# A four-layer decoder on one core: first-pass score tiles stand behind each half of a pair's scores

## What is computed

```python
# layer 0: 32 values a head, layer 1: 64 (four key heads), layer 3: 16
scores = jnp.einsum('bhid,bhjd->bhij', q, k) / sqrt(d)     # layer 0 adds a term for position
att = jnp.where(causal_mask, scores, -inf)
att = jax.nn.softmax(att, axis=-1)
y = jnp.einsum('bhij,bhjd->bhid', att, v)
```

## Time and profile before

| | us |
|---|---|
| three timed runs, median | 3255.83 |
| lowest and highest of them | 3252.84, 3267.48 |
| profiled execution, span (no other time is given for it) | 3262.6 |
| layer 0 attention, stretch 140 to 508 | 368: PE busy 314.55, DVE 239.07 |
| layer 1 attention, stretch 1140 to 1660 | 520: PE busy 415.08, ACT 321.41, POOL 327.25, DVE 276.62 |
| layer 3 attention, stretch 2555 to 2868 | 313: PE busy 266.24, DVE 224.46 |

### The profile page before, as it was taken

One profiled execution on the slowest core, in us unless ns is written; L12 is line 12 of the kernel. 1 busy time (PEld: TensorE's weight loads), 2 busy tenths in 40 slices (PEclk: granted clock), 3 DMA queues, 4 the chain that ended last, 5 costly groups with the idle time before them and its releaser, 6 DMA issues. The chain is left out here.

```text
span 3262.6 us, 45065 instructions
## 1 busy us (share of the span) xinstructions
PE 2508.7 (77%) x15890; PEld 1399.0 (43%) x15890; DVE 1855.3 (57%) x5014; ACT 1480.5 (45%) x2984; POOL 996.1 (31%) x822
## 2 busy tenths in 40 slices
PE   6788885785667577888874669897776788859977
PEld 2323324564443233333352255564443333346666
DVE  6576655565645455555553558335432577656678
ACT  5334451453432156666641514224412355537876
POOL 1145561146347566666612300001101111101200
PEclk9889998897878789999986869997687799978989
DMA  3311101610444411111002210001000322114023
GB/s 112 94 43 42 42 2 36 229 54 19 125 154 101 108 47 46 35 41 46 17 15 67 34 39 1 10 4 30 14 1 33 74 28 28 16 48 123 1 78 104
DMA packets 186942, 174.52 MB, mean 53 GB/s; under 512 B 52777, under 2 KB 160042, under 8 KB 186462
## 3 DMA queue, kind: packets, MB, share of 16 engines
q1 hardware_dynamic: 172030, 153.84, 16.8%
q0 software_dynamic: 9408, 12.56, 2.5%
q10 hardware_dynamic: 5280, 5.24, 0.5%
HBM read 117.62 MB, written 57.40 MB: 54 GB/s over the span
## 5 line engine op out<-in xcount | busy, mean ns | idle before, releaser
L946 POOL TENSOR_TENSOR l1a_p_lo<-res,l1a_p_hi 128x1024 f16<-128x1024 f32 x192 | 311.9, 1643 | 177.2 <-ACT res L1187 177.2
L1196 ACT ACTIVATE l0a_probs<-ps 128x1024 f32<-128x1024 f32 (+1 forms) x192 | 145.5, 810 | 176.2 <-PE ps L1050 103.7
L1196 ACT ACTIVATE l3a_probs<-ps 128x1024 f32<-128x1024 f32 (+1 forms) x192 | 146.9, 809 | 143.3 <-PE ps L1050 116.2
L1186 ACT ACTIVATE l1a_p_hi<-ps 128x1024 f16<-128x1024 f32 x192 | 157.8, 822 | 110.9 <-PE ps L1050 82.8
L1047 PE MATMUL ps<-l1a_qs,l1a_ks 128*128 128x512 f16 (+3 forms) x768 | 167.7, 333 | 31.6 <-ACT res L1187 31.6
L1016 PE MATMUL ps<-l1a_ks,l1a_qs 128*128 128x512 f16 (+3 forms) x384 | 122.2, 347 | 78.7 <-DVE l1a_nmax L1221 33.0
L1218 DVE CUSTOM_DVE_ANT_0 l1a_masked<-ps,l1a_wide_mask 128x128 bf16<-128x128 f32 (+3 forms) x256 | 118.0, 490 | 103.1 <-PE ps L1016 100.9
L971 POOL TENSOR_TENSOR l0a_both<-l0a_probs 128x768 f32<-128x768 f32 (+2 forms) x96 | 154.7, 1633 | 46.3 <-PE ps L1088 46.0
L1187 ACT ACTIVATE res<-ps 128x1024 f32<-128x1024 f32 x192 | 158.1, 823 | 0.0
L1050 PE MATMUL ps<-mask_t,ident_b 128*128 128x128 bf16 x768 | 157.5, 225 | 0.0
L1218 DVE CUSTOM_DVE_ANT_0 l0a_masked<-ps,l0a_wide_mask 128x128 bf16<-128x128 f32 (+3 forms) x256 | 116.5, 489 | 68.0 <-PE ps L1016 67.3
(11 more groups left out here) (749 smaller groups left out, 6453.7 us busy)
## 6 DMA issues: line engine op xcount, KB each, us to landing
f_wf<-in_L_ffn_w_dram SPq DMA_DIRECT2D x16, 1024.0 KB
f_slots<-x0a_zeros SPq DMA_DIRECT2D x32, 256.0 KB, 3.4
f_xe<-f_slots SPq DMA_DIRECT2D x32, 256.0 KB, 3.0
f_ys<-f_y SPq DMA_DIRECT2D x32, 256.0 KB
l1a_qs<-l_q_h SPq DMA_DIRECT2D x64, 128.0 KB
d_wall<-in_L_ffn_W_dram SPq DMA_DIRECT2D x3, 2112.0 KB
l0a_qs<-l_q_h SPq DMA_DIRECT2D x32, 128.0 KB
l0a_ks<-l_k_h SPq DMA_DIRECT2D x16, 256.0 KB
```

Of the source, the lines that this page charges most:

```text
L946: pool.tensor_tensor(ph_lo[:, n % SLOTS, :, 0:w], probs[:, n % FULL, :, 0:w], ph_hi[:, n % SLOTS, :, 0:w], ALU.subtract).then_inc(s_["low_ ...
L1186: act.activation(ph_hi[:, n % SLOTS, :, 0:w], SB[n % 2][:, :, 0:w], ACT.Exp)
L1196: act.activation(probs[0:KR, n % SLOTS, 2 * pr:2 * pr + 2, 0:w], SB[x % 2][:, :, 0:w], ACT.Exp).then_inc(s_["exps"], 1)
```

## The change

A unit now has a place behind each half of each pair of scores (2 x `PR` places), one behind the values unless `split` is set (layer 1), and one behind the sums only where sums come, that is in layer 0 on even units. `scores` gets the items that go between its two halves. In the last unit, which has no scores ahead, the places of both halves are worked off in turn. Nothing is added to or taken from any engine's instructions.

```diff
-    def lay(self, PR, C, ones):
+    def lay(self, PR, C, split, paired):
...
-                parts += [(n, k, 2 * C * w1) for k in range(PR)] + [(n, PR, 4 * w)] + ([(n, PR + 1, 4 * w)] if ones else [])
+                parts += [(n, k, max(C * w1, 1)) for k in range(2 * PR)]
+                if not split:
+                    parts.append((n, 2 * PR, 4 * w))
+                if paired and n % 2 == 0:
+                    parts.append((n, 2 * PR + 1, 4 * w))
...
+    paired = not own_sums and G == 4
+    items, before, beside, rest = plan.lay(PR, C, split, paired)
...
-                def scores(n, pr):
+                def scores(n, pr, between):
...
+                        for a in between if half == 0 else ():
+                            item(a)
...
                     for pr in range(PR):
                         if n + 1 < U:
-                            scores(n + 1, pr)
-                        for a in beside[n][pr]:
+                            scores(n + 1, pr, beside[n][2 * pr])
+                        for a in beside[n][2 * pr + 1] if n + 1 < U else beside[n][2 * pr] + beside[n][2 * pr + 1]:
                             item(a)
...
-                    for a in beside[n][PR]:
+                    for a in beside[n][2 * PR]:
                         item(a)
...
-                    for a in beside[n][PR + 1]:
+                    for a in beside[n][2 * PR + 1]:
                         item(a)
```

More of the change, by code:

```diff
@@ L808, in packed_attention @@
     n_ld = len(stack.q_parts) * GB + len(stack.k_parts) + (GB + 1 if q_pos is not None else 0)
-    items, before, beside, rest = plan.lay(PR, C, not own_sums)
+    paired = not own_sums and G == 4
+    items, before, beside, rest = plan.lay(PR, C, split, paired)
     turned_at = {s: a + 1 for a, (what, s, i) in enumerate(items) if what == "turn"}
@@ L819, in packed_attention @@
     invert_after = [[s for s in range(S) if s + INV < S and plan.first_unit[s + INV + 1] - 1 == n] for n in range(U)]
-    paired = not own_sums and G == 4
     in_reduce = plan.key_rows == P
@@ L1118, in _ @@
                 for pr in range(PR):
-                    scores(0, pr)
+                    scores(0, pr, ())
                 for n in range(U):
```

2 lines of the change are left out of this document (1 added, 1 removed).

## The result

The changed kernel is slower by about 1%: four executions with a median of 3286.99 us (3278.39 to 3302.34) against 3254.34 for the kernel before. The ratio is 1.0095, with a 95% interval of 1.0072 to 1.0118, so +23 to +38 us. The forecast was 3254, with a range up to 3268. The profiled execution is the shortest of the four (3278.39, span 3276.6), and that of the kernel before (span 3262.6) is some 10 us longer than its median, so the traces show less than the medians' 33 us: some 20 us in the four attentions, 14 in the span.

The account below looks back on a forecast made before the run. PE was taken as the fullest engine in the three causal attentions, its waits set by DVE and, in layer 1, also ACT. Layer 0 -7, layer 1 +7, layer 3 -2 made -2 us: 3255.8 to 3254, range 3240 to 3268.

Parts of the forecast that it names:

- the cover in layer 1's first part: Layer 1, odd turn to third tile: PE's path grows 1.2 us, costing nothing while SP's loads run; 1.1 us cover left.
- Rival (2): Layer 1, slower: the covered 2.0 us come through; 2 us a period more than counted gives 3284; chance 0.06.
- bound of 3.0 a period: Layer 1's upper bound if nothing covers: 0.5 + 1.2 + 0.8 + 0.5 = 3.0 us a period, +45 us.
- Second part of layer 1, +0.5: Layer 1, third tile to next odd turn: 0.46 + 0.3 - 0.6 + 0.5 - 0.2 = +0.5 us a period.
- The clock: Layer 1: four of 16 long waits drop the clock, 1.6 us each; half comes back, -3 us.
- Rival (3): Layer 1, slower: the split long wait drops the clock in each period, 11 more drops, 3275; chance 0.06.
- Layer 0, -7: Layer 0: -1.0 us a period over seven periods with tiles to place, -7 us.
- 0.27 + 0.83: Layer 0, gains a period: odd turn 0.27 us earlier, and 0.83 us saved by splitting five tiles behind the short step's values.
- Term (c): Layer 0: four tiles around sums instead of three, and long-step tiles meeting DVE mid-pair; +0.1 us, between 0 and +0.8.
- rival (4): Whole kernel: waits only change place and name because DVE's order and pace stay; 3256 +- 2; shares the forecast's chance 0.70.
- Layer 3, -2: Layer 3: odd turn 0.2 us and even turn 0.13 us earlier, 7 x 0.33 = -2 us, between -6 and +2.
- The tiling mode: Layer 1: a change from values to sums costs 0.1 us; as the only effect, -6 there and 3241 in all.

Follow-up runs that it names:

- run 5: The changed kernel with DVE's inverse ahead of the odd turn's split in layer 1, instead of behind it; 3273.55 us, ratio 1.0049.
- Runs 10: The kernel before, with layer 1's column transfer issued ahead of the last of the nine loads; 3254.40 us, ratio 1.0001.
- 11: The kernel before, with layer 1's column transfer issued ahead of the last three of the nine loads; 3232.16 us, ratio 0.9917.
- run 16: New places in layers 0 and 3, old ones in layer 1, loads behind the even step in all three, not the cross attention; 3213.37 us, ratio 0.9871.
- run 13: The kernel before, with new places only in the short steps of layers 0 and 3; 3254.23 us, ratio 0.9999.
- runs 14: New places in layers 0 and 3, old ones in layer 1, late loads in all three and the cross attention; 3237.54 us, ratio 0.9937.
- run 15: The kernel before with late loads alone, in layers 0, 1, 3 and the cross attention; 3239.71 us, ratio 0.9946.
- run 7: The kernel before, with layer 1's places all behind whole pairs, none behind halves, values or sums; 3305.63 us, ratio 1.0152.
- run 1: New places in layer 1 alone, layers 0 and 3 as in the kernel before; 3281.92 us, ratio 1.0073.
- run 2: New places in layers 0 and 3 alone, layer 1 as in the kernel before; 3250.68 us, ratio 0.9984.

## Why the prediction was wrong, point by point

**The step that failed is the cover in layer 1's first part.** The forecast had PE's path to the third tile grow by 1.2 us and let it cost nothing, because "that tile is released at 14.71 by SP's chain, which starts at the odd turn and is not touched". The path grew by 0.96 in run 5, where the stall is out (the tile at 15.14 us, less its wait of 1.80, against 14.71 less 2.33). But the tile is not released by SP's chain. The columns had landed by then (12.48 us behind the turn in the period shown), and the row that I quoted for them, already says that something else was late: 0.93 us for a sum of 128x8, which takes 0.15 behind the odd turn. It ends with POOL's subtraction, and that follows the exponentials, and they follow the scores ahead of the even turn, which TensorE's order delays. The cover moved along with what it was to cover. Runs 10 and 11 show it in the kernel before. In the changed kernel the rows show the same: the sum ends 0.02 us behind the subtraction in all 13 periods with loads, here in the period of the result (POOL ends at 1400.23, the sum at 1400.26):

```profile
1399.57 0.69 DVE L1249 TENSOR_TENSOR l1a_y_col<-l1a_y_col 128x8 f32<-128x8 f32 x1 [2.33 <-DMA l1a_y_col<-res]
```
```profile
1398.11 2.12 POOL L951 TENSOR_TENSOR l1a_p_lo<-res,l1a_p_hi 128x1024 f16<-128x1024 f32 x1 [2.47 <-ACT res L1194]
```

The table shows the consequence: the second piece of the period is the same to 0.03 us with and without the change. In the forecast's own cut, the first part was to stay at 14.71 us; it measured 15.87, and 15.14 without the stall.

**What the forecast did not have at all is the stall of 0.73 us** behind the odd turn. Its cause was in the sum: the odd turn 0.5 us later, which came out as 0.49. I counted it as half a microsecond on PE and did not ask which other engine's work starts by the clock of the scores and not of the turn. DVE's order was unchanged and so was POOL's, but their order against each other was not.

**The size.** 1.65 us a period by 15 periods are 24.8 us, which is what the profiled layer 1 lost (505.4 to 530.2). The forecast had +7. Rival (2) named the place and the price (2 us a period more than counted, 3284); it got a chance of 0.06 for want of a reason why the cover should fail. That the forecast's own terms with nothing covered, 0.5 + 1.2, come near 1.65 is luck: 0.73 of the loss is the stall, which is in neither. Its bound of 3.0 a period adds the turn's 0.8 to the 1.2, which by its own waits already holds it.

**Second part of layer 1, +0.5.** Cut at the third tile it measured 16.61 against 16.12, which is +0.49. So the sum of that part came out as forecast. But it is only the tile moving: from the even turn on, nothing was lost.

**The clock.** Half of four drops was to come back. Between the odd turns at 1222.67 and 1595.94 before, and 1220.82 and 1615.04 after, lie 12 periods; less 12 times the undisturbed period, drops cost 3.3 us before and 4.4 after. In this stretch there were eight instead of three, each cheaper (in the whole of layer 1's periods nine instead of four). Rival (3) thus had the right sign and a small part of the size, 1.1 us of its 18. Its price was also too high: the four drops of the kernel before made their periods 0.9 to 1.6 us longer, and the forecast read the dearest one.

**Layer 0, -7.** The short step did get shorter, 12.3 instead of 13.4 us, by as much as the 0.27 + 0.83 that I counted, though 0.43 of it is only moved, as follows. The long step got longer, from 27.6 to 28.2 to 29.2 us. Over six periods, odd turns from 225.11 to 471.29 before and from 229.01 to 475.22 after, the time is 246.18 and 246.21: nothing. Term (c), "+0.1, between 0 and +0.8", was the one mis-sized. Three things were not in it. The even turn now stands ahead of the last unit's values (0.43 us by their row), so a part of the gain only changed sides. DVE's waits do not go away when a bunch is taken apart: in the long step from 282.13 to 311.31 seven tiles wait for DVE. And SP's loads stand ahead of the columns in layer 0 as well, so the columns keep their distance from the odd turn: their transfer is issued 8.85 us behind it before (274.93) and 8.79 us now (278.60). With the shorter step the even turn comes before they land, and DVE, which had found them there, stands still for them (the changed kernel, and run 16, where the loads are late):

```profile
284.43 0.25 DVE L1252 RECIPROCAL l0a_r_col<-l0a_y_col 128x16 f32<-128x16 f32 x1 [1.39 <-DMA l0a_y_col<-l0a_sums]
```
```profile
282.93 0.23 DVE L1256 RECIPROCAL l0a_r_col<-l0a_y_col 128x16 f32<-128x16 f32 x1
```

PE's first wait of that long step hangs on it:

```profile
285.76 0.39 PE L1021 MATMUL ps<-l0a_ks,l0a_qs 102*128 102x512 f16 x1 [0.59 <-DVE l0a_nmax L1228]
```

In the six long steps of the changed kernel DVE waits 0.74, 1.39, 1.42, 0.58, 0.69 and 0 us, and they take 28.53, 29.18, 29.21, 28.37, 28.47 and 28.23: each is 27.79 plus the wait, but for the last. In run 13, with the old places in the long step, it is 27.34 plus waits of 0.95 to 1.46, and 28.07 without one. With late loads (runs 14 and 16) DVE never waits there, each of these long steps takes 28.23 or 28.24, and the period is 40.56 to 40.57, against 41.01 with the old places (run 15): of the -1.0 that I counted, 0.45 is left. So with the loads in their old place rival (4) has the right number for this layer, but only a part of the reason. Layer 0 as a whole shows +3.6, but that is its start: the granted clock rises to full at about 188 us before and at about 198 after. Run 5 has the same places in layer 0 and rose at about 189, so the change does not force it (stretch 188 to 192 us of the kernel before, the changed one and run 5). That it makes it likelier is not excluded: with new places there five of eight profiled executions rose at 198, with the old ones none of ten later than 195.

```profile
188.00:192.00 4.00, 3.17 (x30) 1.24 (x22) 2.76 (x11) 1.02 (x2) 2.60 (x2) 1.00 0.00 0
```
```profile
188.00:192.00 4.00, 3.44 (x13) 0.46 (x8) 1.49 (x7) 0.74 (x1) 3.22 (x2) 0.50 0.00 0
```
```profile
188.00:192.00 4.00, 3.01 (x16) 0.61 (x14) 2.21 (x11) 0.98 (x2) 3.58 (x2) 0.87 0.00 0
```

**Layer 3, -2.** Right in sign, and the mechanism is there: the turns' waits for DVE fell from 12.5 us (6.3 and 6.2) to 9.6, while those of masked tiles rose from 6.2 to 7.2. The layer takes 297.8 to 301.9 us in five runs with the new places against 302.0 to 308.3 in nine with the old ones, with the loads in their old place: -4.6 on average. What I passed by there was larger: the row for which the spreads wait lands behind the loads, and late loads take 16 us off the layer (303.6 to 287.9 with the old places, run 15).

**The tiling mode.** The forecast weighed that a change of mode between values and sums costs 0.1 us. In run 7 as in the changed kernel the sums follow the values directly, and run 7 is the slowest of all, so whatever that saves is far below what a wrong place costs; the runs do not show it by itself.

**What stays open.** Of the 33 us between the medians the profiled executions show 20 in the attentions and 14 in the span. Layer 1 alone measured +25 (+15 to +33, run 1), the other layers alone -7 (-10 to 0, run 2); together that is 18 and not 33, which the intervals leave room for and no run explains. Most kernels here scatter by 13 to 28 us from execution to execution, and I could not say which stage the other executions of the changed kernel lost more in.

## What to carry to other kernels

An engine whose instruction order does not change can still be slowed by a change elsewhere: look for DVE instructions with two inputs in SBUF that start during a long POOL instruction or a few tenths of a microsecond ahead of one, and ask which of the two the change moves. When a row takes six times as long as the same row elsewhere in the trace (0.93 and 0.15 us here), find out why before building on what follows it. And before a delay is called covered, follow the cover back to its start: if its chain passes through what is delayed, it covers nothing. The same goes for a gain: in layer 0 a step that got 1.1 us shorter met a transfer that did not come earlier.

## What the runs showed of the hardware

- A tiny DVE instruction with two SBUF inputs (128x8, 0.15 to 0.17 us) that starts during a POOL subtraction of 128x1024 (2.12 us) ends 0.02 to 0.03 us after it, whatever is left of it: 0.29, 0.93, 1.16, 1.46, 1.73 and 1.98 us are all the same instruction or its neighbour. A step with one SBUF input (TENSOR_SCALAR of 128x8, 0.17 us) was hit once in run 11 as well (2.01 us). Starting 0.07 us ahead keeps it at 0.17, and POOL takes 2.12 us in either case.
- One such loss of 1.81 us cost 0.73 us a period, since only part of it reaches PE; an instruction that starts 0.24 us later cost nothing, and one that starts 0.48 us later 0.83 us.
- Nine loads of 128 KB that were moved by one step brought 1.75 us a period, not because they took less time, but because the small transfer behind them then landed ahead of a POOL instruction and not during it.
- The point in time at which the clock came back to its higher level in layer 0 differed between runs with the same places there by up to 12 us (185 to 195 us with the old ones, 186 to 198 with the new ones), and with it the layer by some 2 to 4 us.
